# Attention scores by four 32-row quarters of the TensorE array into four PSUM banks, and a rewritten instruction order, in a two-layer vision transformer

## The reference

```python
# layer 0: attention with 16 heads of 16, rotary positions, causal
q, k = rope(x @ Wq.T), rope(x @ Wk.T); v = x @ Wv.T
attn = softmax(where(causal, -inf, q k^T / 4)); x = x + (attn @ v) @ Wo.T
# layer 0: mixture of 8 experts, 2 of them per row, each two matrices 256->1024->256
# layer 1: attention with 16 heads, 8 value "rules" shared by all heads, mixed per row and head;
#   then Wf, LayerNorm, 256 -> 512 -> relu -> 256
# layer 1: FFN  y = layernorm(gelu(LN(x) @ sign(W_fc).T)) @ sign(W_proj).T  (1024 hidden)
```

## Time and profile before

| | |
|---|---|
| median of 3 runs | 553.65 us (553.48 to 555.54) |
| the profiled execution | 550.58 us; first to last instruction 548.8 us |
| PE busy | 506.9 us (92%) |
| DVE busy | 375.6 us (68%) |
| ACT busy | 272.9 us (50%) |
| POOL busy | 190.5 us (35%) |
| mean granted TensorE clock | 0.993 |

### The profile page before, as it was taken

How to read it: one execution, slowest core, us unless ns; L and a number is a source line. 1 busy time by engine, 2 the same in 40 slices (tenths; PEclk the granted TensorE clock), 3 DMA queues, 4 the chain that set the end, 5 groups by cost and what they waited for, 6 DMA issues and landing times.

```text
span 548.8 us, 12145 instructions
## 1 busy us (share of the span) xinstructions
PE 506.9 (92%) x3902; PEld 426.6 (78%) x3902; DVE 375.6 (68%) x943; ACT 272.9 (50%) x634; POOL 190.5 (35%) x257
## 2 busy tenths in 40 slices
PE   8989999999998878989999999999999989889996
PEld 7878877887877656667778888888888768678885
DVE  4555466546537776565997877878878687668874
ACT  4120322223233363357667677677677886444331
POOL 3232132132234210565555354364363412132330
PEclk9899999999999998999999999999999999999999
DMA  8934432533415000000000000000000000000000
GB/s 301 380 112 155 153 129 85 169 103 102 153 29 176 1 2 1 1 0 2 1 1 2 1 0 0 0 0 0 0 0 1 1 1 1 1 10 26 17 17 24
DMA packets 10990, 29.62 MB, mean 54 GB/s; under 512 B 2192, under 2 KB 3408, under 8 KB 10704
## 3 DMA queue, kind: packets, MB, share of 16 engines
q1 hardware_dynamic: 10960, 29.23, 15.9%
HBM read 27.98 MB, written 1.25 MB: 53 GB/s over the span
## 4 chain that ended last, share of the span: by engine, by line
PE 42%; DVE 6%; issue 5%; ACT 3%; POOL 1%; DVEq 1%; POOLq 0%; ACTq 0%
PE score L2069 6%; PE tb L1808 3%; PE score L1873 3%; PE bz L2099 3%; PE tb L1810 3%; PE tb L1809 3%; PE bank L1810 3%; PE bank L1809 3%; PE bank L1808 3%; PE tb L1891 2%; PE bz L2081 2%; PE bz L1822 1%; PE bz L1808 1%; DVE we_h L1438 1%; PE tb L1822 1%
## 5 line engine op out<-in xcount | busy, mean ns | idle before, releaser
L383 POOL TENSOR_TENSOR h<-h,scaled 114x256 f32 (+1 forms) x88 | 69.1, 785 | 49.9 <-ACT scaled L686 43.3
L335 POOL TENSOR_TENSOR small<-small,half 114x1 f32<-114x1 f32 x44 | 25.8, 586 | 136.5 <-DVE small L969 136.5
L552 ACT ACTIVATE p_exp<-sc,cst 114x608 f32<-114x608 f32 x66 | 48.2, 795 | 25.6 <-DVE sc L1050 25.6
L1923 PE MATMUL bz<-ebuf 128*128 128x256 f32 x256 | 58.7, 382 | 0.0
L560 ACT ACTIVATE pt<-tb 114x456 f32<-114x456 f32 x66 | 34.6, 556 | 36.0 <-PE tb L1891 36.0
L1923 PEld LDWEIGHTS bz<-ebuf 128*128 128x128 f32 x256 | 47.7, 192 | 5.9
L1891 PE MATMUL tb<-cst,p_exp 114*114 114x114 f32 x352 | 44.0, 266 | 6.1 <-ACT pt L560 3.3
L2069 PE MATMUL score<-v,pt 114*114 114x137 f32 x352 | 48.9, 282 | 0.3 <-ACT o L653 0.3
L686 ACT ACTIVATE scaled<-bank,gl 114x256 f32<-114x256 f32 x88 | 39.0, 473 | 17.3 <-PE bank L1810 6.2
L1891 PEld LDWEIGHTS tb<-cst,p_exp 114*114 114x114 f32 x352 | 35.2, 134 | 15.1 <-ACT pt L560 6.7
L2069 PEld LDWEIGHTS score<-v,pt 114*114 114x114 f32 x352 | 44.1, 178 | 2.1 <-issue 0.4
(11 more groups left out here) (218 smaller groups left out, 1349.6 us busy)
## 6 DMA issues: line engine op xcount, KB each, us to landing
ebuf<-in_w_in SPq DMA_DIRECT2D x16, 512.0 KB, 4.3
ebuf<-in_w_out SPq DMA_DIRECT2D x16, 512.0 KB, 5.1
x_raw<-in_x_tiles SPq DMA_DIRECT2D x11, 342.0 KB, 3.0
out<-h SPq DMA_DIRECT2D x10, 114.0 KB
raw<-in_w_a SPq DMA_DIRECT2D x4, 256.0 KB, 4.7
ebuf<-in_fc SPq DMA_DIRECT2D x1, 1024.0 KB, 4.8
ebuf<-in_proj SPq DMA_DIRECT2D x1, 1024.0 KB, 6.9
raw<-in_w_a SPq DMA_DIRECT2D x2, 384.0 KB, 5.7
```

The lines of the kernel that those rows point to most:

```text
L383: gp.tensor_tensor(h[0:R, t, :], h[0:R, t, :], scaled[0:R, e % 4, :], ALU.add).then_inc(moe_acc, 1)
L552: act.activation(p_exp[0:R, :, b * S:(b + 1) * S], sc[0:R], ACT.Exp, bias=cst[0:R, CB + b:CB + b + 1], scale=SCALE).then_inc(exps, 1)
L1923: last = pe.matmul(bz[:, m * D:(m + 1) * D], ebuf[:, 0, c * D + m * P:c * D + (m + 1) * P], ebuf[:, 1, c * D:(c + 1) * D], start=(c == 0 a ...
```

## The change

The array is used in four quarters of 32 rows. A quarter holds 2 heads of 16 rows, so HQ goes from 4 to 2: `k_exp` has half the columns, a matmul takes 32 rows and 76 columns, four quarters write to four banks, and a tile has 24 fp32 score matmuls in place of 12. Since PSUM has eight banks, `tb` becomes banks 2 and 3 of `score`; the Wo product of all tiles but the last goes to the free half of `bk[2]`. As a score matmul now overwrites `tb`, `c2_v`, whose result lies in `tb[0]`, moves ahead of the scores, and `c2_qT` waits for its reading. The order of all engines is rewritten from tile 8 on; in `c_step` also, and the loop `d_step` is gone: all d1/d2 calls are written out among c2 and c3 of tiles 9 and 10. Some waits of d1/d2 are relaxed (`d2_proj` waits for `centred`, not `done`; `d1_gelu` for the previous tile's bn_stats alone). `a_step` keeps its order.

```diff
-HQ = H // 4
+HB = H // 4
+HQ = H // 8
-    c[:, CH:CH + HQ] = p[:, None] % (P // 2) // HD == np.arange(HQ)
+    c[:, CH:CH + HQ] = p[:, None] % (P // 4) // HD == np.arange(HQ)
-        score = ctx.enter_context(nc.psum_tensor("score", [P, 2, 512], F32))
-        tb = [ctx.enter_context(nc.psum_tensor(f"tb{i}", [P, 512], F32)) for i in range(2)]
+        score = ctx.enter_context(nc.psum_tensor("score", [P, 4, 512], F32))
+        tb = [score[:, 2 + i, :] for i in range(2)]
+
+        def wo_place(t):
+
+            return tb[0][0:R, 0:D] if isinstance(t, int) and t == T - 1 else bk[2][0:R, D:2 * D]
...
                 if causal:
-                    for i in range(2):
-                        pe.matmul(score[0:R, i, 0:HF * S], idb[0:R, 0:R], cmask[0:R], start=True, stop=False)
+                    for i in range(4):
+                        pe.matmul(score[0:R, i, 0:HB * S], idb[0:R, 0:R], cmask[0:R], start=True, stop=False)
                 for f in range(2):
                     for b in range(G):
-                        for i in range(2):
-                            rows64 = slice(i * P // 2, (i + 1) * P // 2)
+                        for i in range(4):
+                            rows32 = slice(i * P // 4, (i + 1) * P // 4)
                             last = pe.matmul(score[0:R, i, f * HQ * S:(f + 1) * HQ * S],
-                                             q_exp[rows64, f].rearrange("p b x -> p (b x)")[:, b * R:(b + 1) * R],
-                                             k_exp[rows64, f, :, b * S:(b + 1) * S],
+                                             q_exp[rows32, f].rearrange("p b x -> p (b x)")[:, b * R:(b + 1) * R],
+                                             k_exp[rows32, f, :, b * S:(b + 1) * S],
...
             def c2_v(t):
-                pe.wait_ge(q_ready, 2 * (t + T) + 2)
+                pe.wait_ge(t2["lo"], t + 1)
             def c2_qT(t):
                 pe.wait_ge(qk1_out, t + 1)
+                pe.wait_ge(v1_ready, 2 * t + 2)
...
 # PE, c_step
                 c3_wf(i - 4)
+                c2_v(i - 2)
+                c2_pv(i - 3, (4, 5))
                 c2_qk(i - 2)
-                c2_pv(i - 3, (4,))
                 c1_moe(i - 1, (2,))
                 c2_qT(i - 2)
+                c3_x(i - 4)
+                c1_x(i)
                 c2_kT(i - 2)
-                c2_pv(i - 3, (5,))
-                c1_x(i)
-                c3_x(i - 4)
                 c1_moe(i - 1, (3,))
                 c2_scores(i - 2)
                 c3_r1(i - 4)
                 c1_gate(i)
-                c2_v(i - 2)
+                c1_moe(i, (0,))
                 c3_r1T(i - 4)
-                c1_moe(i, (0,))
-                c2_turn_p(i - 2, (0, 1))
                 c1_moe(i, (1,))
-                c2_turn_p(i - 2, (2, 3))
+                c2_turn_p(i - 2, (0, 1, 2, 3))
                 c3_r2(i - 4)
 # ACT, c_step
-                softmax_exp(i - 2 + T)
-                c3_relu(i - 4, (0, 1, 2, 3))
-                c2_pt(i - 2, (0,))
-                c2_pt(i - 2, (1,))
+                softmax_exp(i - 2 + T, (0, 1, 2))
+                c3_relu(i - 4, (0, 1, 2))
+                c2_pt(i - 2, (0, 1))
+                c3_relu(i - 4, (3,))
+                c2_pt(i - 2, (2, 3))
                 c1_gate(i)
-                c2_pt(i - 2, (2, 3))
# POOL, ahead of c1_add(0): the rstd that stood between it and rstd_pair(0)
+            rstd(n1, 2)
             c1_add(0, (0, 1, 2, 3, 4, 5, 6, 7))
-            rstd(n1, 2)
             rstd_pair(0)
 # PE, d2_proj
                 pe.wait_ge(gT_lo, 2 * t + 2)
-                since(pe, done, t)
+                since(pe, centred, t)
 # PE, the end: where the loop stood (an excerpt)
+            d2_turn(2, (1,))
             c3_r2(9)
+            d2_proj(1)
+            d1_fc(4, (0,))
             c3_att(10)
+            d1_fc(4, (1,))
             c3_wf(10)
+            d2_turn(3, (0,))
+            d1_x(5)
+            d2_turn(3, (1,))
+            d2_proj(2)
+            d1_x(6)
+            d1_fc(5, (0,))
             c3_x(10)
...
-            with pe.Fori(4, T) as i:
-                d_step(i, 0, 3)
-            for i in range(T, T + 3):
-                d_step(i, i - T + 1, 3)
```

More of the change, by code:

```diff
@@ L422, in d2_bias @@
                 gp.tensor_tensor(h[0:R, t, :], h[0:R, t, :], bw[0:R], ALU.add).then_inc(hb_ready, 1)
[L424 to L430, removed]
             split_wc(8)
             split_x(9)
+            rstd(nA, 9)
             a1_rope(8)
             split_x(10)
-            rstd(nA, 9)
             a1_rope(9)
@@ L1641, in _ @@
-            c2_k(2, (0, 1))
             c2_v(2, (0,))
             mix(1, 0)
+            aggr(n4, 0)
+            plus_eps(n4, 0)
+            mix(1, 1)
+            mix(1, 2)
+            normed1(2)
+            c3_normed(0)
+            c2_v(2, (1,))
+            mix(1, 3)
+            mix(1, 4)
+            c2_k(2, (0, 1))
+            c3_x(0)
+            c1_x(4)
+            mix(1, 5)
+            softmax_max(2 + T)
+            softmax_sub(2 + T, (0, 1))
             gate(4, 0)
-            normed1(2)
@@ L1781, in _ @@
             keep_sums()
+            mix(10, 9)
+            d1_norm(4)
+            c3_x(9)
+            mix(10, 10)
+            d1_x(3)
+            d0_stats(5)
+            d2_stats(2, (0,))
+            d2_lo(1, (0,))
+            d2_centre(0)
+            d2_lo(1, (1,))
+            aggr(nD, 5)
+            plus_eps(nD, 5)
+            d2_stats(2, (1,))
+            mix(10, 11)
+            d2_aggr(2)
+            c3_res(9)
+            mix(10, 12)
+            d2_eps(2)
+            d1_x(4)
@@ new lines, in _ @@
+            d2_centre(4)
+            d2_lo(5, (0,))
+            d2_eps(5)
+            aggr(nD, 9)
+            d2_lo(5, (1,))
+            d2_stats(6, (0, 1))
+            d2_out(4)
+            d2_centre(5)
+            d2_aggr(6)
+            plus_eps(nD, 9)
+            d2_lo(6, (0, 1))
+            d2_eps(6)
+            d2_stats(7, (0,))
+            d1_norm(9)
+            d2_stats(7, (1,))
+            d1_x(8)
+            d2_out(5)
+            d2_centre(6)
+            d2_aggr(7)
+            d2_lo(7, (0, 1))
@@ new lines, in _ @@
+            c3_res(10)
+            d2_eps(7)
+            d2_out(6)
+            d0_stats(10)
+            d2_stats(8, (0,))
+            aggr(nD, 10)
+            plus_eps(nD, 10)
+            d1_x(9)
+            d2_stats(8, (1,))
+            d2_centre(7)
+            d1_norm(10)
+            d2_lo(8, (0, 1))
+            d1_x(10)
+            d2_aggr(8)
+            d2_eps(8)
+            d2_out(7)
+            d2_stats(9, (0, 1))
+            d2_centre(8)
+            d2_lo(9, (0, 1))
+            d2_aggr(9)
@@ L2185, in d2_proj @@
                 last.then_inc(proj_mm, 1)
-            def d_step(i, first, last):
-                on = [first <= k <= last for k in range(4)]
-                if on[3]:
-                    d2_turn(i - 3)
-                if on[2]:
-                    d1_fc(i - 2)
-                if on[1]:
-                    d1_x(i - 1)
-                if on[3]:
-                    d2_proj(i - 3)
             scores(7, True)
@@ L2353, in _ @@
+            d2_turn(3, (1,))
+            d2_proj(2)
+            d1_x(6)
+            d1_fc(5, (0,))
             c3_x(10)
+            d1_fc(5, (1,))
+            d2_turn(4, (0, 1))
+            d2_proj(3)
+            d1_fc(6, (0,))
             c3_r1(10)
+            d1_fc(6, (1,))
+            d2_turn(5, (0,))
             c3_r1T(10)
-            c3_r2(10)
-            with pe.Fori(4, T) as i:
-                d_step(i, 0, 3)
-            for i in range(T, T + 3):
-                d_step(i, i - T + 1, 3)
+            d1_x(7)
@@ new lines, in _ @@
+            d2_turn(5, (1,))
+            d2_proj(4)
+            d1_fc(7, (0, 1))
+            d1_x(8)
+            d2_turn(6, (0, 1))
+            d2_proj(5)
+            c3_r2(10)
+            d2_turn(7, (0,))
+            d2_proj(6)
+            d2_turn(7, (1,))
+            d1_x(9)
+            d1_fc(8, (0, 1))
+            d2_proj(7)
+            d2_turn(8, (0, 1))
+            d1_fc(9, (0,))
+            d1_x(10)
+            d1_fc(9, (1,))
+            d2_proj(8)
+            d2_turn(9, (0, 1))
```

926 lines of the change are left out of this document (496 added, 430 removed).

## The result

The kernel after takes 551.96 us (median of 16 runs, 550.40 to 553.17), the kernel before 553.66 us beside it. The ratio is 0.9972, 95% interval [0.9958, 0.9985]: 1.5 us faster, within the 0.5% that I called no change. I predicted 538.5 us and a range of 528 to 551. The profiled execution took 551.9 us, with a span of 550.1 us where that of before had 548.8.

The account below looks back on a forecast made before the run. PE was taken to bound the C loop, a DVE, ACT and POOL chain the rest. Terms -2.2 - 2.5 - 2.5 + 1.2 - 9.0 = -15.0 from 550.58, plus 3.07 for the median, gave 538.5 us, range 528 to 551.

Parts of the forecast that it names:

- 1, the score matmuls: Score matmuls in every tile: 0.10 us per group of four, 0.36 us less per tile; k_exp 0.24 us shorter.
- A: Rival: score quarters run at their columns' speed, 0.063 us per group, 6 us less, 532; chance 0.12.
- D: Rival: only two quarters' weights load at a time, 0.20 us per group, 565; chance 0.06.
- 2, layer 0 to tile 7: Layer 0's first 8 tiles: DVE sets the gain, 0.27 us per tile, 2.2 us less.
- 3, tiles 8 to 10: Layer 0's tiles 8 to 10: 3 x 0.36 from matmuls, 3 x 0.5 from half the waits filled; 2.5 us less.
- 4, the start of layer 1: Layer 1's tiles 0 to 2: rstd moved away, shorter k_exp wait, faster scores; 2.5 us less.
- 5, the C loop: C loop, 6 PE-bound passes: scores give 0.36 us, a turn_p stall costs 0.5; 1.2 us more in all.
- 6, the tail: From 405 us on: d1/d2 pieces fill c3's waits; three quarters of 11.2 us, 9 us less.
- The sign I had set: Profile sign for the tail: after the C loop no wait of PE of over 1 us.
- The clock: Whole kernel: granted clock 0.993, taken not to matter after the start; no term in the sum.
- Rival B: The tail gives little, waiting for DVE's order, or the C loop loses 0.5 us and more per pass; 546; chance 0.22.
- E: Rival: a wait of the new orders inside a loop costs 2 us a pass; 551 to 556; chance 0.07.

Follow-up runs that it names:

- e1: Kernel after with its new order of work, but the scores by two halves of 64 rows again: 559.49 us, ratio 1.0119.
- e7: Kernel after with idle matmuls (5, 2 and 5) ahead of waits at 49 and 257 to 259 us: 548.96 us, ratio 0.9935.
- e4: Kernel after with the second half of the first tile's Gelu moved right behind the first half, 6 table loads instead of 8: 548.73 us, ratio 0.9938.
- e5: e4 with tile 1's Gelus also moved behind the Exp of tile 10's mixing, and their statistics later, 4 table loads: 548.64 us, ratio 0.9923.
- e10: Kernel after up to the C loop's end, then the kernel before's tail with the value product ahead of the scores: 560.45 us, ratio 1.0126.
- e11: Kernel before with the second half of tile 0's Gelu moved between Exps, 6 table loads instead of 4: 555.53 us, ratio 1.0057.

## Why the prediction was wrong

**1, the score matmuls: right.** 0.10 us per group of four, 0.36 us per tile, and e1 finds them worth 8.1 us in the whole, with the shorter masking of keys. Rivals A and D are out. `k_exp` took its 0.39 us in layer 0 and 0.45 in layer 1, 0.24 less in both.

**2, layer 0 to tile 7: right in kind, a little large, and hidden by the clock.** A pass is 19.5 us (19.4 forecast, 19.7 before). e7 reaches tile 7 at 166.3 us, 3.1 us sooner than before. From the first scores on, where both profiles have the full clock, that is 1.7 us, against 2.2 forecast; the other 1.4 lie ahead of them, where the kernel before has a fall of its own. The kernel after is there at 169.8: the fall at 50 us took 3.3 of a step.

**3, tiles 8 to 10: too large by 1.4.** 1.1 us came, which is the matmuls' 3 x 0.36. The half of the waits that I had filled was not: the scores of tiles 8 and 9 wait 1.18 and 1.19 us, now for `k_exp`, where they waited 1.08.

**4, the start of layer 1: the sign was wrong.** +2.1 us, of which a fall of the clock is 2.1 (21.2 us against e7's 19.1). Even in e7 this stretch is 0.2 us longer than before, where 2.5 less were forecast. Tile 2's wait for its keys did go. But PE now waits for the Exps of tiles 0 and 1, where it did not before; its timeline of e7:

```profile
241.98 0.99 PE L2011 MATMUL score<-cst,p_exp 114*114 114x114 f32 x8 [0.86 <-ACT p_exp L571]
...
261.02 0.99 PE L2011 MATMUL score<-cst,p_exp 114*114 114x114 f32 x8 [0.90 <-ACT p_exp L571]
```

Tile 2's step is 21.1 us where it was 20.3, with no wait over 0.25 us in it; no run shows what the 0.8 us are.

**5, the C loop: right**, 21.2 us, with the stall where I put it, though its removal gave back 0.3 us a pass and not 0.5.

**6, the tail: the step that failed.** "I take three quarters, 9 us" was 1.1 us, and that much the score matmuls alone give: with halves the tail is 143.9 us (e1). The sign I had set, no wait of PE over 1 us behind the C loop, failed too: there are waits of 1.39 and 1.28 us for Gelu's output. I counted PE's waits and VectorE's load, and of ScalarE only that it answers. Two things were left out. The dealt-out Gelus bring four table loads: 3.5 us (e4, e5). And the term counted idle time of the old order as if quarters could have that order; under the shared banks the old order itself is 8 us longer in the one adaptation tried, half-rate stretches included (e10). That the new order spends its gain on what the banks demand fits this and is not shown. Of the 4.4 us that remain short after the loads the cause stays open: in e5 PE still waits 2.1 us for Gelu's output in two places, 1.0 us for `attT` and 1.0 us in three places for VectorE's copies of the transposed Gelu output. The last D tiles are 5.7 us apart, as forecast (530.30 to 535.97 us).

**The clock: no term of the sum.** I wrote that it does not matter after the start. At like clocks the change is worth more than the medians say: at 0.981 the three executions of before average 557.0 us and the one of after has 553.0; at 0.987 fourteen average 554.0 and the one of after has 551.9. Some 2 us of the forecast went there: 2.0 by e7's runs, and 2.5 by the mean clocks, 0.990 and 0.984, at the 0.45 us per 0.001 given below. Why the kernel after has the lower clock is not shown.

Rival B named the right place (the tail gives little) with the wrong reason, and E's number came out without a wait inside a loop, so by luck. What I did not price is a cost of the layout on the order: two halves of one change, each seen as a gain.

## What to carry to other kernels

When work is dealt out among other work on ScalarE, write down the table of each function in the new order and count the changes; each was worth 0.6 to 0.9 us of a tail here. When a change shares a resource (here PSUM banks) to save on the bound engine, price the old order under the new sharing first: the saving was 8 us, and the order that came with it gave back 6.6, the table loads among it. And where PE waits for a microsecond, look at the granted clock behind it, in more than one profile: with 12 idle matmuls the runs were 2.0 us shorter, though a pair of profiled executions says 5.4.

## What the runs showed of the hardware

- Four fp32 matmuls of 32 rows on the four row quarters start within 20 ns and the next four 0.10 us later, for 76 columns and 114 columns of weights; two of 64 rows with 152 columns took 0.13 us (1.82 us for 12 pairs, drain included).
- A load of ScalarE's function table takes 1.28 us each time between Exp and Gelu; Relu, copies and Identity run behind either without one.
- The granted clock of the same kernel differs from execution to execution (0.981 to 0.997 before), and its time with it: by a line through the 54 executions 0.45 us per 0.001.
- Half-rate stretches of 3 to 7 us came behind waits of 0.8 to 1.4 us and during one of 4.49 us (e11), and not behind all waits of that size: of two executions with the same program up to there and the same wait of 0.82 us at 50 us, one has the fall (e11) and one has not (before).
